# Four normalisation groups with their root chains dealt out, logits one block behind, and a looser update wait in a gated linear attention

## The reference

```python
x = x + 0.5 * _L0_ffn_ref(_layernorm(x), ...)      # layer 0: top-1 expert layer
x = x + _L0_attn_ref(_layernorm(x), ...)           # layer 1: gated linear attention
x = x + 0.5 * _L0_ffn_ref(_layernorm(x), ...)      # layer 2: as layer 0
x = x + 0.5 * _L1_ffn_ref(_layernorm(x), ...)      # layer 3: top-2 experts
x = x + _L1_attn_ref(_layernorm(x), ...)           # layer 4: gated attention unit
x = x + 0.5 * _L1_ffn_ref(_layernorm(x), ...)      # layer 5: as layer 3
```

```python
q = silu(x @ Wq.T); f = sigmoid(x @ Wk.T); log_f = log_sigmoid(f); k = 1.0 - f; v = x @ Wv.T
def step(S, inp):
    S = exp(g_t)[..., :, None] * S + k_t[..., :, None] * v_t[..., None, :]
    o_t = einsum('bhk,bhkv->bhv', q_t, S)
out = rmsnorm(out, norm_w) @ Wo.T
```

## Time and profile before

| | before |
|---|---|
| median of the runs | 1283.04 us (1280.93 to 1285.11) |
| the profiled execution's own time | 1278.25 us |
| its span | 1276.1 us |
| TensorE matmul busy | 672.3 us (53%) |
| VectorE busy | 738.6 us (58%) |
| ScalarE busy | 489.5 us (38%) |
| GpSimd busy | 553.1 us (43%) |
| mean granted TensorE clock | 0.778 of full |

### The profile page before, as it was taken

How to read it: one execution, slowest core, us unless ns; L and a number is a source line. 1 busy time by engine, 2 the same in 40 slices (tenths; PEclk the granted TensorE clock), 3 DMA queues, 4 the chain that set the end, 5 groups by cost and what they waited for, 6 DMA issues and landing times.

```text
span 1276.1 us, 20751 instructions
## 1 busy us (share of the span) xinstructions
PE 672.3 (53%) x5982; PEld 544.7 (43%) x5983; DVE 738.6 (58%) x2301; ACT 489.5 (38%) x1079; POOL 553.1 (43%) x538
## 2 busy tenths in 40 slices
PE   4210582466646111870659999127777448999100
PEld 4210451245635000550648888014445337889100
DVE  6682354767884850547354556339985764556222
ACT  5300232544435000331507788126555206788000
POOL 2117563044440045561236666654311126663575
PEclk9999996679875555885558999668878659999655
DMA  9401313000000002213102334111000102335232
GB/s 294 120 8 46 92 57 92 1 1 0 0 3 1 1 27 80 72 43 90 50 23 68 76 82 67 49 43 34 25 17 9 34 15 67 77 81 71 61 82 68
DMA packets 86769, 67.78 MB, mean 53 GB/s; under 512 B 10522, under 2 KB 78362, under 8 KB 86706
## 3 DMA queue, kind: packets, MB, share of 16 engines
q1 hardware_dynamic: 72978, 38.99, 10.7%
q0 software_dynamic: 13728, 28.02, 9.4%
HBM read 38.53 MB, written 28.44 MB: 52 GB/s over the span
## 4 chain that ended last, share of the span: by engine, by line
PE 36%; DVE 26%; POOL 13%; issue 12%; ACT 6%; DMA 3%; another core or an unknown queue 3%; DVEq 0%; POOLq 0%; ACTq 0%; SPq 0%
POOL rt L1106 6%; POOL xslots L1080 5%; PE bank L619 4%; PE bank L640 4%; PE bank L621 3%; PE bank L643 3%; PE bank L620 3%; DVE rt L800 3%; PE bank L641 3%; PE bank L391 2%; DVE stats L352 2%; DVE x L983 2%; PE bank L603 1%; DVE turned L931 1%
## 5 line engine op out<-in xcount | busy, mean ns | idle before, releaser
L1065 POOL DMA_INDIRECT turned<-xrows_moe,token x156 | 168.7, 1081 | 144.1 <-DVE token L900 60.7
L702 ACT ACTIVATE turned<-bank,b1T 128x256 f32<-128x256 f32 x312 | 122.4, 475 | 111.4 <-PE bank L621 93.8
L1106 POOL DMA_INDIRECT rt<-y_moe,slot_i x128 | 122.7, 959 | 87.7 <-issue 37.2
L931 DVE TENSOR_TENSOR turned<-turned 128x1024 bf16<-128x1024 f32 (+1 forms) x118 | 125.3, 1062 | 34.9 <-ACT turned L706 18.5
L640 PE MATMUL bank<-w2h,turned 128*128 x780 | 141.0, 224 | 4.6 <-DVE turned L931 2.3
L641 PE MATMUL bank<-w2h,turned 128*128 x780 | 141.0, 224 | 1.0 <-issue 1.0
L619 PE MATMUL bank<-rt,w1h 128*128 128x256 bf16 (+1 forms) x468 | 126.3, 270 | 26.3 <-issue 11.1
L1080 POOL DMA_INDIRECT xslots<-xn,slot_i x64 | 69.4, 1084 | 163.1 <-DVE slot_i L865 144.2
L942 DVE COPY arena<-bank 128x256 f32<-128x256 f32 x118 | 49.8, 422 | 141.2 <-remote 89.9
L620 PE MATMUL bank<-rt,w1h 128*128 128x256 bf16 (+1 forms) x468 | 125.5, 268 | 0.0
L621 PE MATMUL bank<-rt,w1l 128*128 128x256 bf16 (+1 forms) x468 | 125.2, 268 | 0.0
(11 more groups left out here) (302 smaller groups left out, 1835.4 us busy)
## 6 DMA issues: line engine op xcount, KB each, us to landing
y_moe<-arena SPq DMA_DIRECT2D x78, 128.0 KB
turned<-xslots SPq DMA_DIRECT2D x18, 256.0 KB
arena<-y_moe SPq DMA_DIRECT2D x16, 256.0 KB, 4.7
xslots<-xn SPq DMA_DIRECT2D x5, 512.0 KB, 6.0
turned<-xrows_moe,token POOLq DMA_INDIRECT x156
x<-in_x SPq DMA_DIRECT2D x4, 512.0 KB, 5.9
arena<-in_w SPq DMA_DIRECT2D x1, 2048.0 KB, 9.4
turned<-in_w SPq DMA_DIRECT2D x8, 256.0 KB, 4.4
```

Of the source, the lines that this page charges most:

```text
L702: last = nc.scalar.activation(s["h32"][:, k % 2, o], bank[1 + 2 * (k % 2) + u // 2][:, W * (u % 2):W * (u % 2) + W], ACT.Gelu, bias=b1T[:, ...
L931: nc.vector.tensor_tensor(s["hl16"][:, k % 4], s["h32"][:, r], s["hh"][:, k % 4], ALU.subtract)\
L1065: nc.gpsimd.indirect_dma_start(out=s["xs"][:, 2 * (t % BODY) + j], out_offset=None, in_=s["xdram"], in_offset=bass.IndirectOffsetOnAxis(ap ...
L1106: nc.gpsimd.indirect_dma_start(out=ytok[:, at % TOK], out_offset=None, in_=s["ydram"], in_offset=bass.IndirectOffsetOnAxis(ap=slot_i[:, k, ...
```

## The change

- All norms of layers 1, 2 and 3 have four groups of eight tiles.
- The chain of a group becomes a generator that yields after each step. `combine` (and the additions behind the attention) take one step of the previous group's chain behind each addition and each statistics instruction; what is left over follows in one piece. In layer 1 the copies and low halves of a group are ordered copy, copy, low, copy, low, ..., those of blocks 0 and 1 between groups 2 and 3, those of blocks 2 to 4 behind the last group with steps of the last chain between, and those of blocks 5 to 7 after that chain.
- TensorE makes logits (or queries) of block i-1 behind the turning of block i, in all four layers.
- In layer 1's loop the update waits for "dve" (with a credit) instead of "state", which only the second output matmul waits for; key and value are copied in one ScalarE instruction, as soon as the keys are turned; the sums of squares go to a column of their own and are copied once per batch.

```diff
+        def moments_by_steps(dve, s, g):
...
+            dve.wait_ge(*s.at("stat", b))
+            done(nc.vector.tensor_tensor(one(0), st(1), st(4), ALU.add))
+            yield
...
+            for i in range(NEWTON):
+                dve.wait_ge(q, n)
+                done(nc.vector.tensor_tensor(t, y, y, ALU.mult))
+                yield
...
+            copy(blocks[0])
+            for i in blocks[1:]:
+                copy(i)
+                low(i - 1)
+            low(blocks[-1])
...
-                if i >= 2:
-                    after(i - 2)
-            after(NS - 2)
+                if i >= 1:
+                    after(i - 1)
             return after(NS - 1)
...
+            for g in range(1, last + 1):
+                chain = moments_by_steps(dve, next_ln, g - 1)
+                for quad in range(groups[g][0] // QUAD, groups[g][1] // QUAD):
+                    combine(dve, s, quad, count, chain)
+                finish_steps(chain)
+                if next_ln["halves"] and 2 <= g < last:
+                    a, b = groups[g - 2]
+                    ln_halves(dve, next_ln, range(a // TPS, b // TPS))
+            chain = moments_by_steps(dve, next_ln, last)
+            open_from = groups[last][0] // TPS - 1
+            if next_ln["halves"]:
+                ln_halves(dve, next_ln, range(groups[last - 2][0] // TPS, open_from), chain)
+            finish_steps(chain)
+            if next_ln["halves"]:
+                ln_halves(dve, next_ln, range(open_from, NS))
...
-                    nc.tensor.transpose(kv[:, 0:P], ga["k"][:, k, c], ident)
+                    nc.tensor.transpose(kv[:, 0:P], ga["k"][:, k, c], ident).then_inc(gl["kv"], 1)
...
-                    pe.wait_ge(gl["state"], n + 1)
+                    pe.wait_ge(gl["dve"], n + 1)
...
+                    pe.wait_ge(gl["state"], n + 1)
                     nc.tensor.matmul(O[:, 0:P], state, ga["qT"][:, tok], start=False, stop=True).then_inc(gl["st2"], 1)
...
-                    nc.tensor.matmul(Y[:, P:P + 1], ga["sq"][:, i % 2], ones_f[:, 0:1], start=True, stop=True)\
+                    nc.tensor.matmul(Y[:, P + i:P + i + 1], ga["sq"][:, i % 2], ones_f[:, 0:1], start=True, stop=True)\
...
-                    act.wait_ge(gl["st1"], n + 1)
+                    act.wait_ge(gl["kv"], n + 1)
...
+                    nc.scalar.activation(ga["ktv"][:, i % 2], bank[2 + i % 2][:, 0:2 * P].rearrange("p (a f) -> p a f", a=2),
+                                         ACT.Copy).then_inc(gl["act1"], 1)
...
+                    if i == CH - 1:
+                        copy = nc.scalar.activation(ga["ss"][:, ds(CH * b, CH)], bank[6][:, P:P + CH], ACT.Copy)
+                    copy.then_inc(gl["ycopied"], 1)
...
-        ln1 = layernorm(x, xn, [8, 24], halves=True)
-        ln2 = layernorm(x, xn, [8, 8, 16])
+        ln1 = layernorm(x, xn, [8, 8, 8, 8], halves=True)
+        ln2 = layernorm(x, xn, [8, 8, 8, 8])
...
-        ln3 = layernorm(x, xn, [8, 24])
+        ln3 = layernorm(x, xn, [8, 8, 8, 8])
```

More of the change, by code:

```diff
@@ L354, in ln_moments, with finish_steps @@
+        def finish_steps(chain):
+            for _ in chain:
+                pass
         def ln_moments(dve, s, g):
@@ L360, in ln_moments, with ln_halves, copy @@
             nc.vector.memset(credit[:, 30:31], 0.0).then_inc(s["scal"], 1)
-        def ln_halves(dve, s, blocks):
-            for i in blocks:
+        def ln_halves(dve, s, blocks, chain=iter(())):
+            def copy(i):
                 o = slice(NMAX * i, NMAX * (i + 1))
@@ L367, in ln_halves, with low @@
                 nc.vector.tensor_copy(xnT[:, o], bank[i % 2][:]).then_inc(s["copied"], 1)
+                next(chain, None)
+            def low(i):
+                o = slice(NMAX * i, NMAX * (i + 1))
                 dve.wait_ge(*s.at("copied", i + 1))
@@ L988, in combine @@
                     next_stats([t])
+                    next(chain, None)
         def combine_all(dve, s, next_ln=None):
[L992 to L1003, removed]
+            if next_ln is None:
+                for quad in range(NT // QUAD):
+                    combine(dve, s, quad, None)
+                return
+            count = lambda tiles: ln_stats(next_ln, tiles)
+            groups = next_ln["groups"]
+            last = len(groups) - 1
+            for quad in range(groups[0][1] // QUAD):
+                combine(dve, s, quad, count)
+            for g in range(1, last + 1):
[13 more added lines that the diff above has]
+                ln_halves(dve, next_ln, range(open_from, NS))
         def fill_sync(sp, ln):
@@ L1384, in gla_vector @@
                     ln_stats(next_ln, [t])
-                ln_moments(dve, next_ln, g)
+                    next(chain, None)
+                finish_steps(chain)
+                chain = moments_by_steps(dve, next_ln, g)
+            finish_steps(chain)
         NJ = L // P
```

59 lines of the change are left out of this document (49 added, 10 removed).

## The result

| | before | after |
|---|---|---|
| median of five runs each, same chip | 1283.92 us (1280.93 to 1290.85) | **1268.49 us** (1267.82 to 1273.67) |
| ratio, with its 95% interval | | 0.9888 (0.9866 to 0.9909) |
| span of the profiled execution | 1276.1 us | 1266.2 us |
| mean granted TensorE clock | 0.778 | 0.780 |

The forecast was 1269.6 us in 1262 to 1276.

A forecast was written before the change was run, and what follows sets the result against it. No engine bounds the whole; each stage has its own limit. 5.7 + 4.9 + 1.6 + 3.3 - 2.1 = 13.4 us, taking the profiled 1278.25 to 1264.9 and, from the median 1283.04, giving 1269.6, range 1262 to 1276.

The forecast's parts named there:

- Price of a dealt step, 0.08 us: VectorE in the norms: a small step between large independent instructions costs 0.08 us, against 0.20 when waiting for the previous step.
- Rival (a): Norms of three layers: dealt steps drain VectorE, 144 steps at 0.2 us make it 28 us dearer, 1297; chance 0.05.
- The Trainium skill's rule: VectorE: the next operation waits until the pipe is empty; a dealt step costs 0.17 us, the sum 2.6 us.
- Layer 2, 5.7: Layer 2's norms: four groups with dealt chains permit blocks 4 and 5 earlier, TensorE then limits; gain 5.7 us.
- Layer 3, 4.9: Layer 3's norms: the same regrouping, but two GpSimd splits meet VectorE at 2.5 us each; gain 4.9 us.
- Rival (c): More collisions with GpSimd: a third group's split, or full 3.2 us each, 1272 to 1274; chance 0.08.
- Layer 0, 1.6: End of layer 0: only the logit order changes, two blocks instead of three behind the last turning; gain 1.6 us.
- Layer 1, a loss of 2.1: Layer 1's norms: the last chain's 13 steps come late behind low 4, ScalarE waits 3 us; loss 2.1 us.
- The loop, 3.3: Layer 1's loop: 1.2 us inside batches, 2.0 over three batch boundaries, 0.1 at the last end; gain 3.3 us.
- (b): Layer 1's loop gives nothing, as GpSimd and VectorE carry it: 1272.9 us; chance 0.16.
- (d): Norms of layers 2 and 3: TensorE's clock rises to 2.4 GHz, some 4.5 us less each, 1260.6; chance 0.04.
- (e): Layer 1's norms do not lose but gain 1.2 us: 1266.3; chance 0.10.

The follow-up runs named there:

- after_again: The changed kernel run again without any edit, on a faster chip; ratio 0.9886 to the kernel before on the same chip.
- no_deal: The changed kernel with each group's chain of small steps in one piece instead of dealt out; 1282.82 us, ratio 0.9979.
- rows_early: The changed kernel with GpSimd's row work for the third block moved ahead of its loop work; single run, 1214.67 us against 1225.79 for the kernel before.
- wait_only: The kernel before with only the looser wait of the state's update, key and value still in two copies; single run, 1280.95 us against a median of 1284.45.
- best: The changed kernel plus VectorE's new order in layer 1, late GpSimd splits in layer 3 and early GpSimd row work; 1203.96 us against 1227.96 before, ratio 0.9805.
- before_again: The kernel before run again without any edit, on a faster chip; ratio 1.0011 to the kernel before on the same chip.

## Why the prediction was right

- **Price of a dealt step, 0.08 us.** Right, in all three layers. Rival (a), the drain, is out. The Trainium skill's rule on it (page "VectorE: DVE Perf Modes", section "The DRAIN you can't avoid") is not what these rows show; what they fit is the exception that the same section adds and that I left out, that a next operation that is not held starts earlier. My 2.6 us for the sum under that rule was also a slip: 144 steps at 0.085 more each leave 13.4 - 12.2 = 1.2. The permits of layer 2 came 9.3, 14.9, 20.5 and 23.8 us behind the first addition, where I had 9.4, 15.3, 21.2 and 24.7: a group cost 5.6 us, where I added up 5.8 and then used 5.9, and the last chain 3.35 instead of 3.5.
- **Layer 2, 5.7.** Measured 6.4. The path was the one named: the third permit lets block 4 go, and from its turning on TensorE is the limit. The third permit came 0.7 us earlier than reckoned; TensorE took 11.7 us from block 4's turning, where I had 11.5.
- **Layer 3, 4.9.** Measured 5.0 and 5.3, with exactly two meetings. They cost 2.8 and 2.7 us in after (the second and third permits came 17.7 and 26.0 us behind the first addition, in layer 2 14.9 and 20.5) and 2.5 and 2.7 in after_again, where I took 2.5. Rival (c) didn't come, though no_deal shows how near it lay.
- **Layer 0, 1.6.** 1.7: from the end of the last normalisation to the last logit it is 6.5 us in all five profiles with the old order of logits and 4.8 in all nine with the new one.
- **Layer 1, a loss of 2.1.** Measured 1.9 and 1.6, ScalarE idle for 3.17 us where I had 3. The step that lost was the one named. That the last silu ended 44.2 us behind the first addition, to the tenth as forecast, is luck: the last permit came 34.5 us behind it, not 35.5, and from there it took 9.7 us, not 8.7, at a granted clock of 0.64, where before.py's last two blocks had 1.00.
- **The loop, 3.3.** The size was near, the reason half wrong. At full clock the edits give 0.6 us at each of three batch ends (I had 0.65) and 0.1 three times inside a batch (I had 1.2 in all): 2.1. I put the batch end down to the sums' copy; it comes from the looser wait (0.52 of 0.6). Inside a batch I had 0.7 for the first batch, where TensorE is slower, and 0.17 for each of the others: 0.4 to 0.9 at a clock of 0.85, and 0.1, bear that out. On average the four profiles with the old loop took 110.8 us and the six with both new edits and GpSimd's rows where they were 107.6: 3.2 less. Of the 1.1 beyond the 2.1 some 0.5 is chance: two of those four and one of those six have a batch end at a clock of 0.75 to 0.76, 1.3 to 1.4 us longer. The rest is not settled. The 5.35 of the first pair is no measure of the edit: its profile of before had a batch end at 14.14 us and clock 0.76.
- **Together** 6.4 + 5.2 + 1.7 + 3.2 - 1.8 = 14.7 us (13.6 with the loop at 2.1), against 15.4 by the medians and 13.4 forecast. The number is as near as it is partly by luck: the norms gave 1.4 us more than forecast, and the loop 1.2 less at full clock. Rivals (b), (d) and (e) are out: the loop gained, TensorE worked 11.7 us without a gap in layer 2 and the granted clock stayed at 0.50, and layer 1 lost until its order was changed.

## What to carry to other kernels

Small dependent steps are dear in a row (0.20 us each) and cheap between large independent instructions (0.08): taking the dealing out again cost 12.4 us in the three norms, 2.8 of it by a third meeting with GpSimd and part by order in layer 1, of some 14.7 that the whole change gave. When a chain is dealt out, look at what its last steps queue behind; here finishing it first, with two copies moved forward, turned a loss of 2 us into a gain of 4. Look for small VectorE steps that last as long as a GpSimd instruction beside them, in stages that you don't edit too: in layer 0 they set the end 7.5 us later in one profile of the kernel before than in the other. Judge an edit of 1% by the length of its stage at equal granted clock, in several profiles, and not by one pair of spans.

## What the runs showed of the hardware

- A VectorE step of 128x8 that starts beside GpSimd's 128x1024 cast or subtraction lasts as long as that does: 1.04 beside 1.04 and 2.08 beside 2.18 us, for 0.15 alone. Beside the 128x2048 subtractions of layer 0 it lasts 3.9 to 4.0 us. Steps with one tensor input are caught too: a multiplication by a constant took 2.00 us in no_deal (line 376, 128x8), the state's scaling by two values per row 1.69 and 1.81 us in after (0.35 in rows_early). The Trainium skill, page "SBUF — State Buffer", section "Who interferes with whom", has such a port pair that GpSimd and VectorE hold in turn and exclusively; the traces agree, and the size to reckon with here is 2.5 to 2.8 us per split of 128x1024.
- A batch end of the new wait, the last of the loop aside, took 12.5 to 12.6 us at a granted clock of 1.00 and 13.8 (wait_only, no_deal) or 14.2 (best) at 0.75 to 0.76; one of the old took 13.1 and 14.4. That is at least 1.3 us, twice what the edit saves there.
- TensorE worked without a gap for 11.7 us in layer 2's norms (56 matmuls of 128 and 8 columns, after), and for 18.3 in layer 3's before the change, at a granted clock of 0.50 throughout.
- A stretch without any edit differed by up to 5.7 us of some 610 between executions of different kernels, and layer 0's last permit by 9 us (7.5 between before and before_again, the same kernel on two chips), for the reason shown above.
